# Summing the weighed chunks of a side scan by accumulating DMAs in place of VectorE additions

## The chip, the cores and the metric

The kernel runs on one core of a Trainium2 chip. The metric is the device time of one execution in microseconds (us); lower is better. All arrays are float32 unless it says otherwise.

## What is computed

Two layers on x of shape (8, 512, 128). Each is `x = x + s * silu(g)`, with s and g from the normalised x. In layer 0, s is a selective scan and g a mixture of eight experts, of which each token takes two. In layer 1, s is plain causal attention and g is a block with 16-head latent attention and another mixture of experts. The change touches the scan alone:

```python
z = sigmoid(x @ Wz + bz);  x_ssm = x @ Wx + bx
Bm = x @ WB + bB;  C = x @ WC + bC             # 16 states each
dt = softplus(x @ Wdt + bdt);  A_bar = exp(dt[..., None] * -exp(A_log))
x_db = x_ssm[..., None] * (dt[..., None] * Bm[..., None, :])
def ssm_step(h, inp):                          # over the 512 positions
    a_t, x_t, c_t = inp
    h_new = a_t * h + x_t
    y_t = einsum('bdn,bn->bd', h_new, c_t)     # the sum over the states
    return h_new, y_t
s = (y_ssm * z) @ Wout + bout
```

## The kernel before

The kernel has three stages. `route` normalises x, picks the experts and sorts tokens to them. `experts0` runs the experts of layer 0 over NT = 72 tiles of 128 tokens. `layer1` runs the whole second layer as a hand-written schedule of slots, 24 for each of the 8 batches; in every slot each engine finds by its loop what is due.

The scan of layer 0 is a side job, spread by hand over the stages that have other work. Batches 0 to 2 (SCANNED = 3) are scanned inside `experts0`, batches 3 to 7 inside `layer1`, shortly before layer 1 needs each of them. Features lie on the 128 partitions and positions along the row. A chunk is PER = 2 of the 16 states, so a batch has NC = 8 chunks, each a tile of 128 x 1024 float32, which is 512 KB. In `experts0` a chunk comes every three tiles, in `layer1` every four slots.

One chunk k of batch b takes these steps, with n = 8 b + k:

- GpSimd issues two loads (`load_rows`, L212) that spread the rows of B and of C from DRAM (`scan_bc`) over all partitions into `sc_bc_wide`, which has two buffers. The load for chunk n waits until chunk n-2 has used its rows.
- ScalarE makes the decays `sc_a` (L250).
- VectorE multiplies `sc_u` by the B rows into `sc_ub` (`enter`, L291), runs the recurrence into `sc_state` (`step`, L298), multiplies the state by the C rows (`weigh`, L308) and adds the product to the running sum `sc_y` (`add`, L315). The weighed chunk goes into `sc_ub`, which is free after the recurrence; that of chunk 0 goes straight to `sc_y`. The `enter` of the next chunk therefore waits for the `add` of this one.
- After the last chunk `gate` adds the two halves of `sc_y` (L320) and multiplies by the gate (L323). TensorE projects (L196), and `finish` (L327) takes the rows.

In `experts0` VectorE goes through tile m in this order: four products that give `hid` (L908), then `finish`, `add` of the chunk that is due three tiles back, `enter` of the chunk due now, `step` of the one due a tile back, `weigh` of the one due two tiles back. TensorE does the up projections of tile m (L767), the pieces of the scan, the down projections of tile m-2 (L776 and L778, which wait for `hid`), then turns the rows of tile m+2 (L758). SP fetches the expert weights of each tile (`wst`, 512 KB from `in_wexp` and 4 KB from `bias_cols`) into five buffers. GpSimd gathers the rows of the tiles (`xrow`, L885), eight tiles ahead, and issues the loads of the scan between them.

In `layer1` VectorE begins each slot with the maxima of one group of scores (`reduce_maxima`, L1676). TensorE's next scores (L1256, L1259) wait for these, since there is one bank pair for them. After it come the pieces of the scan and then whatever else is due. GpSimd issues the loads, the gathers of expert outputs (L1630) and small roots. SP issues small copies between the engines' steps: `q_all<-q_kind`, `dens<-o`, `rec_wide<-head_recips`.

## Time and profile before

| | us |
|---|---|
| median of 3 runs | 1355.73 |
| lowest, highest | 1346.55, 1360.17 |
| span of the profiled execution | 1355.0 |

| stage | from, to (us) |
|---|---|
| `route` and the start of `experts0` | 0 to 84 |
| `experts0` with the scan of batches 0 to 2 | 84 to 334 |
| end of `experts0`, start of `layer1` | 334 to 376 |
| `layer1` with the scan of batches 3 to 7 | 376 to 1116 |
| `layer1` without a scan | 1116 to 1355 |

The profile comes from one execution, whose own time is its span of 1355.0 us; the time around the span isn't given apart from it. The engines are PE (TensorE), PEld (its weight loads), DVE (VectorE), ACT (ScalarE), POOL (GpSimd) and SP. The chain that ended last is followed back from the end of the program. It does not go back beyond 345 us, where a barrier ends `experts0`; the first stages are read from waits and busy times instead.

### The profile page before, as it was taken

How to read it: one execution, taken by the hardware profiler on the slowest of the kernel's cores; microseconds unless marked ns; L12 is line 12 of the kernel's file. 1: busy time of each engine (PE TensorE's matmuls, PEld its weight loads, DVE VectorE, ACT ScalarE, POOL GpSimd, SP SyncE). 2: the span in 40 equal slices, each digit the busy share in tenths (PEclk: the TensorE clock that was granted, in tenths of full speed). 3: DMA queues.
4: the chain of work that ended last, by engine and by line, in shares of the span. 5: the costliest groups of instructions: out<-in, count | busy, mean ns of one | idle time of the engine just before them, and what ended most of it. 6: DMA issues, size and time to landing. Idle time of an engine off the chain costs nothing.

```text
span 1355.0 us, 21646 instructions
## 1 busy us (share of the span) xinstructions
PE 1197.1 (88%) x7528; PEld 720.3 (53%) x7528; DVE 989.3 (73%) x1648; ACT 641.1 (47%) x1309; POOL 282.1 (21%) x363
## 2 busy tenths in 40 slices
PE   7679989899778889898899989999989998998986
PEld 6568878788334334435544553553454455454353
DVE  6748877979487777986797896699889776653333
ACT  3657758575225334355336544454533533443421
POOL 1075434340303103202020320130032301000000
PEclk9779999999787689899799997999999988998799
DMA  7489978877253252253135323435333400310020
GB/s 196 159 279 295 297 238 285 276 254 230 102 125 96 70 117 85 86 115 101 60 95 134 109 76 86 115 98 105 105 93 95 125 25 18 56 41 18 17 49 8
DMA packets 99674, 167.06 MB, mean 123 GB/s; under 512 B 26216, under 2 KB 54448, under 8 KB 99504
## 3 DMA queue, kind: packets, MB, share of 16 engines
q1 hardware_dynamic: 76624, 89.37, 24.4%
q0 software_dynamic: 22784, 76.04, 18.0%
q8 instruction: 63, 1.03, 0.3%
q10 hardware_dynamic: 160, 0.26, 0.2%
q14 instruction: 43, 0.35, 0.1%
HBM read 141.37 MB, written 11.15 MB: 113 GB/s over the span
## 4 chain that ended last, share of the span: by engine, by line
PE 42%; DVE 17%; issue 6%; ACT 4%; DMA 4%; POOL 1%; SPq 0%; another core or an unknown queue 0%; DVEq 0%; POOLq 0%; ACTq 0%
PE bank L1219 9%; PE bank L1237 4%; PE bank L1256 4%; PE bank L1348 3%; PE bank L1295 3%; PE bank L1290 3%; PE bank L1286 3%; DVE neg_max L1676 3%; PE bank L1222 3%; PE bank L1259 2%; DVE sc_state L298 2%; PE bank L1277 2%; DMA rec_wide<-head_recips 2%; ACT probs L1486 1%; DVE sc_ub L291 1%
## 5 line engine op out<-in xcount | busy, mean ns | idle before, releaser
L1676 DVE TENSOR_REDUCE neg_max<-bank 128x2 f32<-128x1024 f32 (+3 forms) x256 | 204.2, 819 | 160.9 <-PE bank L1259 154.6
L1486 ACT ACTIVATE probs<-bank 128x1024 f32<-128x1024 f32 (+1 forms) x192 | 168.9, 880 | 316.9 <-PE bank L1222 290.6
L1219 PE MATMUL bank<-q_all,kk 49*128 49x512 f32 (+3 forms) x1024 | 221.8, 512 | 21.8 <-ACT probs L1486 18.9
L212 POOL DMA_DIRECT2D sc_bc_wide<-scan_bc x128 | 73.3, 574 | 496.3 <-DVE sc_ub L291 234.7
L767 PE MATMUL bank<-xcol,wst 128*128 128x128 f32 x1152 | 144.9, 280 | 1.6 <-DMA wst<-bias_cols 1.5
L298 DVE TENSOR_TENSOR_SCAN sc_state<-sc_a,sc_ub 128x1024 f32<-128x1024 f32 x64 | 145.9, 2280 | 0.0
L1256 PE MATMUL bank<-kr,q_all 48*128 48x512 f32 (+3 forms) x512 | 111.0, 430 | 33.5 <-DVE neg_max L1676 32.1
L767 PEld LDWEIGHTS bank<-xcol,wst 128*128 128x128 f32 x1152 | 138.3, 197 | 2.8 <-DMA wst<-bias_cols 2.8
L1219 PEld LDWEIGHTS bank<-q_all,kk 49*128 49x128 f32 x1024 | 81.4, 194 | 107.7 <-issue 54.1
L885 POOL DMA_INDIRECT xrow<-sorted_in,token_of x72 | 92.8, 1289 | 154.8 <-PE bank L758 105.9
L908 DVE SCALAR_TENSOR_TENSOR hid<-bank,wst,gel 128x128 f32<-128x128 f32 x288 | 80.3, 341 | 42.2 <-issue 40.3
L1256 PEld LDWEIGHTS bank<-kr,q_all 48*128 48x128 f32 x512 | 50.0, 192 | 104.5 <-DVE neg_max L1676 49.1
L1222 PEld LDWEIGHTS bank<-mask_t,ident 128*128 128x128 bf16 x512 | 29.4, 98 | 122.6 <-issue 115.4
L1237 PE MATMUL bank<-probs,vaug 128*32 128x512 f32 (+3 forms) x1024 | 94.4, 465 | 0.0
L836 ACT ACTIVATE gel<-bank,wst 128x128 f32<-128x128 f32 x288 | 81.5, 383 | 18.3 <-PE bank L767 17.6
L291 DVE TENSOR_TENSOR sc_ub<-sc_u,sc_bc_wide 128x1024 f32<-128x1024 f32 x64 | 78.0, 1218 | 15.4 <-DMA sc_bc_wide<-scan_bc 13.5
L250 ACT ACTIVATE sc_a<-sc_dt,neg_a 128x511 f32<-128x511 f32 x128 | 83.8, 710 | 5.8 <-PEq L680 5.3
L778 PE MATMUL bank<-w,hid 128*128 x576 | 84.9, 291 | 0.0
L1630 POOL DMA_INDIRECT expert_out<-sorted_out,slot x64 | 72.4, 1132 | 47.0 <-POOLq L138 26.9
L1259 PE MATMUL bank<-mask,ident 128*128 128x128 bf16 x512 | 75.8, 232 | 0.0
L1222 PE MATMUL bank<-mask_t,ident 128*128 128x128 bf16 x512 | 74.9, 229 | 0.0
L778 PEld LDWEIGHTS bank<-w,hid 128*128 128x128 f32 x576 | 71.0, 194 | 4.9
(295 smaller groups left out, 1834.8 us busy)
## 6 DMA issues: line engine op xcount, KB each, us to landing
sc_bc_wide<-scan_bc POOLq DMA_DIRECT2D x128, 512.0 KB
wst<-in_wexp SPq DMA_DIRECT2D x72, 512.0 KB
q_all<-q_kind SPq DMA_DIRECT2D x94, 128.0 KB, 4.4
rec_wide<-head_recips SPq DMA_DIRECT2D x31, 256.0 KB
p_t<-gates_turned SPq DMA_DIRECT2D x14, 512.0 KB
sorted_out<-xrow SPq DMA_DIRECT2D x7, 576.0 KB
rows_all<-in_x SPq DMA_DIRECT2D x8, 256.0 KB, 5.0
sorted_in<-rows_all SPq DMA_DIRECT2D x8, 256.0 KB, 5.8
```

The costliest lines, as they stand in the source:

```text
L291: self.nc.vector.tensor_tensor(v["ub"][:], v["u"][:].unsqueeze(1).to_broadcast([P, PER, L]), v["bc_wide"][:, n % 2, 0, :, :], ALU.mult).th ...
L298: self.nc.vector.tensor_tensor_scan(merged(v["state"][:]), merged(v["a"][:, n % 2, :, :]), merged(v["ub"][:]), 0.0, ALU.mult, ALU.add).the ...
L767: last = mm(bk(inner(m)[half])[:, f * P:(f + 1) * P], wst[:, m % WB, half * FF + f * P:half * FF + (f + 1) * P], xcol[:, m % 3, :], start= ...
L778: last = mm(bk(5)[:, 0:P], hid[:, m % 4, f, :], w2[:, bass.ds(e * FF + f * P, P)], start=False, stop=(f == FT - 1))
L885: nc.gpsimd.indirect_dma_start(out=xrow[:, m, :], out_offset=None, in_=xs[0:B * L], in_offset=bass.IndirectOffsetOnAxis(ap=t["token_of"][: ...
L1219: mm(bank[1][:, par, at:at + n], kk[rows, b % 2, kt * P:(kt + 1) * P], q_all[rows, quad // 2 % 3, pair, kt * P:L].bitcast(F32), start=True ...
L1222: last = mm(bank[1][:, par, at:at + P], t["ident16"][:], t["mask_t16"][:], start=False, stop=True)
L1237: last = mm(bk(4)[row:row + 32, kt * P:L], vaug[:, b % 2, kt, :], probs[:, (6 * quad + 2 * kg + pr) % RING, par, at:at + L - kt * P], star ...
L1256: mm(bank[0][:, par, at:at + n], q_all[rows, quad // 2 % 3, pair, i * P:(i + 1) * P], kr[rows, b % 2, 0:n], start=True, stop=False)
L1259: last = mm(bank[0][:, par, at + i * P:at + n], t["ident16"][:], t["mask16"][:], start=False, stop=True)
L1486: af(probs[:, slot % RING, :, 0:width], bank[1][:, :, 0:width], ACT.Exp, scale=0.125).then_inc(s["p_ready"], 1)
L1676: last = v.tensor_reduce(neg_max[:, quad % 2, pr:4:2, i], bank[0][:, :, at:at + (i + 1) * P], AX, ALU.max, negate=True)
```

## The change

For chunks 1 to 6 of every batch (ADDED = NC - 2 = 6) VectorE no longer adds. GpSimd issues a DMA that reads the weighed chunk and accumulates it into `sc_y`, in SBUF on both sides, 512 KB each (`accumulate`). Chunk 0 still writes `sc_y` directly. Chunk 7 is still added by VectorE (`add_last`), which waits for its product and for all six DMAs of the batch.

The weighed chunk gets a tile of its own, `sc_weighed`, so `enter` waits only for the recurrence of the chunk before. In turn `weigh` of chunk k, for k of 2 and up, waits until the DMA of chunk k-1 has landed (`sc_acc`), and each DMA waits for the one before it.

Place in GpSimd's order: in `experts0` behind the load of the C rows in the iterations 11 tiles after a chunk is due; GpSimd waits there for the `weigh` of that chunk. In `layer1` behind the load of the C rows in the slot where VectorE weighs the chunk one slot earlier in the schedule (`chunk_due(slot, 3)`).

To make room, three small tiles of `route` are laid over `sc_weighed`, and `turned_rows` in `layer1` is halved by packing.

```diff
+ADDED = NC - 2
@@ def scan_tiles
-        ub=sb("ub", [P, PER, L]), state=sb("state", [P, PER, L]), ...
+        ub=sb("ub", [P, PER, L]), weighed=sb("weighed", [P, PER, L]), state=sb("state", [P, PER, L]), ...
@@ def enter
         if k == 0:
             dve.wait_ge(s["sc_u"], b + 1)
-            if b >= 1:
-                dve.wait_ge(s["sc_add"], (NC - 1) * b)
-        if k == 1:
+        if n >= 1:
             dve.wait_ge(s["sc_scan"], n)
         dve.wait_ge(self.rows_in[0][n % 2], 16 * (n // 2 + 1))
-        if k >= 2:
-            dve.wait_ge(s["sc_add"], (NC - 1) * b + k - 1)
@@ def weigh
+        if k >= 2:
+            dve.wait_ge(s["sc_acc"], 16 * (ADDED * b + k - 1))
         dve.wait_ge(self.rows_in[1][n % 2], 16 * (n // 2 + 1))
-        to = v["ub"] if k >= 1 else v["y"]
+        to = v["weighed"] if k >= 1 else v["y"]
@@
-    def add(self, dve, b, k):
+    def accumulate(self, pool, b, k):
         s, v = self.s, self.v
-        dve.wait_ge(s["sc_hc"], b * NC + k + 1)
+        pool.wait_ge(s["sc_hc"], b * NC + k + 1)
         if k >= 2:
-            dve.wait_ge(s["sc_add"], (NC - 1) * b + k - 1)
-        self.nc.vector.tensor_tensor(v["y"][:], v["y"][:], v["ub"][:], ALU.add).then_inc(s["sc_add"], 1)
+            pool.wait_ge(s["sc_acc"], 16 * (ADDED * b + k - 1))
+        pool.dma_start(v["y"][:], v["weighed"][:], accum_op=ALU.add).then_inc(s["sc_acc"], 16)
+
+    def add_last(self, dve, b):
+        s, v = self.s, self.v
+        dve.wait_ge(s["sc_hc"], NC * (b + 1))
+        dve.wait_ge(s["sc_acc"], 16 * ADDED * (b + 1))
+        self.nc.vector.tensor_tensor(v["y"][:], v["y"][:], v["weighed"][:], ALU.add).then_inc(s["sc_add"], 1)
@@ experts0, gpsimd
                         if (at := chunk_due(m - after)) is not None and at >= (0, 2):
                             scan.load_rows(pool, *at, what)
+                    if (at := chunk_due(m - 11)) is not None and 1 <= at[1] <= ADDED:
+                        scan.accumulate(pool, *at)
@@ experts0, vector
-                    if (at := chunk_due(m - 3)) is not None and at[1] >= 1:
-                        scan.add(dve, *at)
-                        if at[1] == NC - 1:
-                            scan.gate(dve, at[0])
+                    if (at := chunk_due(m - 3)) is not None and at[1] == NC - 1:
+                        scan.add_last(dve, at[0])
+                        scan.gate(dve, at[0])
@@ layer1, gpsimd
                             scan.load_rows(pool, *at, what)
+                    if (at := chunk_due(slot, 3)) is not None and 1 <= at[1] <= ADDED:
+                        scan.accumulate(pool, *at)
@@ layer1, vector
-                    if (at := chunk_due(slot, 3)) is not None and at[1] >= 1:
-                        scan.add(dve, *at)
+                    if (at := chunk_due(slot, 3)) is not None and at[1] == NC - 1:
+                        scan.add_last(dve, at[0])
```

## Rows read from the trace of the kernel before

**Rows 1.** Busy time by stage: us, engine busy (instructions), PEclk, DMA share, GB/s.

```profile
core 0: us, PE busy (x) PEld busy (x) DVE busy (x) ACT busy (x) POOL busy (x), PEclk, DMA share, GB/s
84.00:334.00 250.00, 231.28 (x1829) 209.23 (x1828) 205.77 (x377) 174.58 (x497) 110.06 (x108) 0.99 0.86 275
...
376.00:1116.00 740.00, 670.56 (x4010) 339.28 (x4008) 597.47 (x848) 332.97 (x556) 135.68 (x178) 0.91 0.37 97
```

**Rows 2.** The additions, groups of VectorE instructions by line, whole program.

```profile
L315 DVE TENSOR_TENSOR sc_y<-sc_y,sc_ub 128x1024 f32<-128x1024 f32 x56 | 68.0, 1214 | 0.0
```

**Rows 3.** Waits between 80 and 343 us: us in total, times, longest.

```profile
DVE sc_ub L291 <- DMA sc_bc_wide<-scan_bc: 13.5, 1, 13.5
...
PE bank L758 <- DVE sc_rows L327: 5.4, 2, 2.7
...
PE bank L776 <- DVE hid L908: 3.8, 3, 1.4
...
PE bank L767 <- DMA wst<-bias_cols: 1.5, 2, 1.4
```

**Rows 4.** Waits over the whole program, longest in total first.

```profile
PEld bank L1256 <- DVE neg_max L1676: 49.1, 40, 3.7
...
PE bank L1256 <- DVE neg_max L1676: 32.1, 26, 3.5
```

**Rows 5.** Additions and batch ends on the chain that ended last: start, us.

```profile
444.30 1.13 DVE sc_y L315
...
692.39 1.22 DVE sc_y L315
...
802.65 1.22 DVE sc_y L315
...
809.90 0.61 DVE sc_y L320
...
1033.27 1.22 DVE sc_y L315
```

**Rows 6.** DMA in 84:334: queue rows, then issues with KB each.

```profile
DMA packets 36557, 68.73 MB, mean 275 GB/s; under 512 B 12829, under 2 KB 20893, under 8 KB 36524
...
q1 hardware_dynamic: 27727, 39.74, 48.7%
q0 software_dynamic: 8797, 28.58, 36.6%
...
wst<-in_wexp SPq DMA_DIRECT2D x67, 512.0 KB
sc_bc_wide<-scan_bc POOLq DMA_DIRECT2D x44, 512.0 KB
```

**Rows 7.** Short stretches of `experts0`, columns as in the first group.

```profile
80.00:86.00 6.00, 6.00 (x43) 5.81 (x43) 3.63 (x6) 2.64 (x11) 4.79 (x6) 0.80 1.03 381
...
194.00:206.00 12.00, 12.00 (x100) 11.10 (x99) 11.90 (x22) 6.85 (x22) 6.67 (x7) 1.00 0.91 289
```

**Rows 8.** A lone 512 KB load, KB and median us to landing.

```profile
c_wq<-in_wq SPq DMA_DIRECT2D x1, 512.0 KB, 4.1
```

**Rows 9.** VectorE between 84 and 165 us: start, us, line.

```profile
107.90 1.22 DVE L308 TENSOR_TENSOR sc_ub<-sc_state,sc_bc_wide 128x1024 f32<-128x1024 f32 x1
...
116.78 1.21 DVE L308 TENSOR_TENSOR sc_ub<-sc_state,sc_bc_wide 128x1024 f32<-128x1024 f32 x1
...
129.66 1.21 DVE L308 TENSOR_TENSOR sc_ub<-sc_state,sc_bc_wide 128x1024 f32<-128x1024 f32 x1
...
133.14 1.23 DVE L291 TENSOR_TENSOR sc_ub<-sc_u,sc_bc_wide 128x1024 f32<-128x1024 f32 x1
```

**Rows 10.** GpSimd's loads of the scan in `experts0`: start, us.

```profile
110.78 0.58 POOL L212 DMA_DIRECT2D sc_bc_wide<-scan_bc  x1
113.93 0.60 POOL L212 DMA_DIRECT2D sc_bc_wide<-scan_bc  x1
```

**Rows 11.** VectorE in `layer1`, two successive weighings of the scan: start, us.

```profile
688.29 1.22 DVE L308 TENSOR_TENSOR sc_ub<-sc_state,sc_bc_wide 128x1024 f32<-128x1024 f32 x1
...
708.63 1.22 DVE L308 TENSOR_TENSOR sc_ub<-sc_state,sc_bc_wide 128x1024 f32<-128x1024 f32 x1
```

**Rows 12.** The chain between 450 and 550 us, shares of the stretch by line.

```profile
by line: PE bank L1219 12.1%; issue 7.0%; PE bank L1256 6.5%; PE bank L1237 5.4%; DMA rec_wide<-head_recips 5.1%; DMA q_all<-q_kind 4.4%; PE bank L1259 4.2%; DMA dens<-o 4.2%; DVE neg_max L1676 3.5%; PE bank L1222 3.3%; DVE sc_state L298 3.
```

More of the change, by code:

```diff
@@ L172, in scan_tiles @@
         bc_wide=sb("bc_wide", [P, 2, 2, PER, L]),
-        ub=sb("ub", [P, PER, L]), state=sb("state", [P, PER, L]), y=sb("y", [P, PER, L]), rows=sb("rows", [P, 3, J, P]))
+        ub=sb("ub", [P, PER, L]), weighed=sb("weighed", [P, PER, L]), state=sb("state", [P, PER, L]), y=sb("y", [P, PER, L]), rows=sb("rows", [P, 3, J, P]))
 def merged(t):
@@ L351, in route @@
         rstd = sb("r_rstd", [P, T])
-        prob, left = sb("r_prob", [P, T, E]), sb("r_left", [P, T, E])
+        early = t["scan"]["weighed"][:].rearrange("p a b -> p (a b)").rearrange("p (n i e) -> p n i e", n=4, i=T)
+        prob, left, firsts = early[:, 0], early[:, 1], early[:, 2:4]
         small = sb("r_small", [P, T, 4])
-        firsts, order = sb("r_firsts", [P, 2, T, E]), sb("r_order", [P, E])
+        order = sb("r_order", [P, E])
         picked = sb("picked", [P, T, E])
@@ L896, in _ @@
                             scan.load_rows(pool, *at, what)
+                    if (at := chunk_due(m - 11)) is not None and 1 <= at[1] <= ADDED:
+                        scan.accumulate(pool, *at)
             @block.vector
@@ L1018, in layer1 @@
         neg_max = sb("neg_max", [P, 2, 4, J])
[L1019 to L1021 removed]
+        turned_rows = sb("turned_rows", [32 + J * E, L])
+        neg_max_t = turned_rows[0:4 * J, 0:2 * P].rearrange("p (q w) -> p q w", q=2)
+        gates_t, gates_rows = turned_rows[32:32 + E, :], turned_rows[32:32 + J * E, 0:P]
         probs = sb("probs", [P, RING, 2, L])
@@ L1622, in _ @@
                             scan.load_rows(pool, *at, what)
+                    if (at := chunk_due(slot, 3)) is not None and 1 <= at[1] <= ADDED:
+                        scan.accumulate(pool, *at)
                     if (b := due(slot, "gather")) is not None:
```

7 lines of the change are left out of this document (2 added, 5 removed).

## The prediction

> **What bounds the kernel now.** I read the busy time by stage first. Between 84 and 334 us TensorE is busy 231.3 of 250 us and VectorE 205.8, and the DMA engines 0.86 of the time [rows 1]. A clean stretch shows who sets the pace: in 12 us TensorE is busy all 12.00 and VectorE 11.90 [rows 7]. So TensorE bounds this stage, VectorE is all but level with it, and the DMA engines are not far off. Between 376 and 1116 us TensorE is busy 670.6 of 740 us, VectorE 597.5, the DMA engines only 0.37 [rows 1]. After 1116 us there is no scan, and nothing of the change reaches it.
>
> Next the waits, which say who holds TensorE up. In the first stage it waited for VectorE 5.4 us at the end of a batch and 3.8 us for `hid`, and 1.5 us for weights [rows 3]. Over the whole program its scores waited 32.1 us, 26 times, for VectorE's maxima; the weight loads' 49.1 us lie partly over the same gaps [rows 4]. That is what relief of VectorE can buy.
>
> Last the chain that ended last. It runs through seven additions between 444 and 1033 us, each 1.13 or 1.22 us [rows 5]. One of them, at 802.65, is the last of its batch, since the sum of the halves (L320) follows at 809.90. That one stays on VectorE, so six leave the chain.
>
> **What the change removes.** 48 of the 56 additions at 1.214 us [rows 2], 58.3 us of VectorE. Of these 18 fall into `experts0` (21.9 us) and 30 into `layer1` (36.4 us). All that VectorE has behind an addition starts 1.2 us sooner, where VectorE is late.
>
> In `experts0` TensorE is the bound, so the gain is at most its waits for VectorE, 5.4 + 3.8 = 9.2 us [rows 3], and at least nothing. The larger item lies at the batch ends, where the addition stays. I take 3 us.
>
> In `layer1` the six additions on the chain are 5 x 1.22 + 1.13 = 7.2 us. If VectorE had been on the path throughout its waits, the gain could reach the 32.1 us of [rows 4]; if TensorE is right behind, it falls towards nothing. Additions just off the chain help a little in the same crowded stretches. I take 10 us, near the chain's own count.
>
> **What it adds on the DMA engines.** 48 DMAs of 512 KB, SBUF to SBUF. The trace has no accumulating DMA. From below: the fastest stretch moves 381 GB/s [rows 7], at which 0.524 MB take 1.38 us of all 16 engines. From above: an accumulate reads the source, reads the destination and writes it. If those passes follow each other, it is three times that, 4.1 us. I take two passes, 2.75 us, as the writing can run beside the reading, and keep both ends.
>
> The Trainium skill bears on the value, in "Collectives: The Full Stack", section "The bandwidth ceiling: the fold count and why AG ≠ RS ≠ AR": an add in the DMA engine is slow because it reads two sources, and a reduce there ran at 32.35 GB/s beside 62.28 for a copy. By its ratio of 1.93 an accumulate would take an estimated 2.66 us here, and the sum would be lower by 18 x 0.09 = 1.6 us at the most. No row of this trace shows it.
>
> In `experts0`: the 68.73 MB of 84 to 334 us [rows 6] need 180 us at 381 GB/s, and 18 x 2.75 = 50 us come on top: 230 of 250 us. On average it fits; the point where it no longer does is (250 - 180) / 18 = 3.9 us each. A chunk has 250 / 24 = 10.4 us, and needs 180 / 24 + 2.75 = 10.3. A clean chunk is shorter: TensorE does 100 matmuls in 12 us [rows 7], some 25 or 26 a tile, so three tiles are 9.4 us. There the engines are 0.9 us short. Were every one of the 18 chunks clean, that would be 16 us; the gaps around them and five weight buffers absorb part.
>
> A rule of the skill speaks against the change here. "DMA: Bandwidth & Descriptors", section "Issuing engines are not separate DMA queues", says that DMAs from any engine end on the same 16 DMA engines and interleave. By it GpSimd's additions can't slip past the weights. By that rule the shortfall above is due, and the trace agrees as far as it can: the two queues hold 48.7% and 36.6% of the same 16 engines.
>
> **The waits it adds.** `weigh` of chunk k waits for the DMA of chunk k-1. In the tight case a weighing ends at 107.90 + 1.22 = 109.1 and the next begins at 116.78, which leaves 7.7 us; the next pair has 129.66 - 118.0 = 11.7 us [rows 9]. A lone 512 KB load took 4.1 us to land [rows 8]; with a second reading of 1.38 us it is 5.5. That fits alone. With the weights taking half the engines it can double to some 10, about 2 us late in the tight chunks. Behind a late `weigh` on VectorE stand `hid` of the next tiles and then TensorE's down projections, two tiles on. VectorE has 1.2 us more slack in each chunk, so I count half of it: 1 us in half of the 18 chunks is 9 us at the most. Shortfall and late waits are the same contention; together I take 7 us (from 0 to 16).
>
> GpSimd itself waits for the weighing: after the load at 110.78 until 118.0. Behind it stand two gathers, eight tiles ahead, and the load now at 113.93 [rows 10], which would go at some 120. Its rows are used at 133.14 [rows 9], so 13 us remain where 19 were. It needs the addition's 2.75, its own 1.4 and 2.7 of latency, 6.9 us, or 11 when shared. I cost this at nothing; what hides it is the two buffers. SP's queue is passed by nothing.
>
> In `layer1` two weighings are 20.3 us apart [rows 11], so the DMA has 19 us to land, and it stands behind a load that waits for the same weighing: no new wait on GpSimd. Its 30 x 2.75 = 83 us lift the DMA share from 0.37 to 0.48. The price is collision with small copies on the chain: they are 5.1 + 4.4 + 4.2 = 13.7% of it in one stretch [rows 12]. If each of the 30 delays such a copy by its whole length whenever one is there, that is 30 x 0.137 x 2.75 = 11 us; queues share, the chain has this density only in places, and the loads of 512 KB do the same already. I take 2 us (0 to 11). The issue on GpSimd is like a load's 0.6 us [rows 10], 29 us on an engine that is busy 110 of 250 and 136 of 740 us [rows 1]. The looser wait of `enter` and the packed tiles cost and bring nothing.
>
> **The sum.** 1355.0 - 3 + 7 - 10 + 2 = 1351.0 us, made against the span of the profiled execution, which is 0.7 us below the median of the runs, so it needs no correction.
>
> **The rivals.**
>
> *The relief is larger (0.26).* The accumulate costs little more than a copy, 1.38 us: then `experts0` needs 180 + 25 = 205 of 250 us and waits for nothing. VectorE's backlog in the crowded parts of `layer1` shrinks by more than the chain counts. For it: seven chain additions are only those that ended last. With 9 us in `experts0` and 18 in `layer1` (a little over half of the 32.1) the time is 1328 us. Against it: TensorE is busy over 90% anyway.
>
> *The accumulate is slow (0.32).* If one takes more than the 3.9 us worked out above, the DMA engines become the bound of `experts0`, and `weigh` waits in each chunk. At 6 us, 180 + 18 x 6 = 288 us, which is 38 us over the stage's 250; with `layer1` at 10 - 4 = 6 us better, the time is 1387 us. It is past 1% slower from about 5 us each. For it: no row shows an accumulate, and my upper end of 4.1 us is already past the point. Against it: the stage has gaps, and two readings at copy speed stay below.
>
> *About no change (0.42).* My forecast, from 1342 to 1368 us: relief and contention nearly cancel. It also holds the case in which TensorE takes up at once what VectorE frees.
>
> **How the numbers follow.** The likeliest gives 1351. A measurement of this kernel can tell about 1% (14 us) from no change. The range of 1330 to 1385 us takes in nearly all of the large relief and of the slow accumulate, and leaves about 2 in 10 outside. Faster by over 1%: 0.26, within 1%: 0.42, slower by over 1%: 0.32.
>
> **What would show it.** In the changed profile: VectorE's busy time down by 58 us; GpSimd with 48 more issues of 0.6 us or so; the DMA share of `experts0` up from 0.86 to near 1, and of `layer1` to about 0.48. The price of one accumulate shows in the packets of GpSimd's queue. A wait "DVE L308 <- DMA sc_y" in the tight chunks of `experts0` and none in `layer1` would bear out the deadlines. `experts0` should be 4 us longer and `layer1` 8 us shorter. I am wrong if such waits stand in `layer1`, if TensorE waits for weights for more than a few us, or if TensorE's 32.1 us for the maxima hardly move.

## The result

The changed kernel takes 1376.7 us in the median of 4 runs (1373.4 to 1380.2); beside it the kernel before took 1354.0 us (4 runs, 1346.6 to 1360.2). The ratio is 1.018, with a 95% interval from 1.013 to 1.023. The change makes the kernel about 25 us slower. That lies inside the wide range of 1330 to 1385 us, near its upper end, but the forecast was 4 us faster and the likeliest case about no change; both were wrong. The prediction had given 0.32 to "slower by over 1%".

The page of the changed kernel, its span, VectorE's and GpSimd's busy time, the DMA queue that GpSimd issues and the shares of the chain that ended last:

```profile
span 1378.4 us, 21646 instructions
...
PE 1202.7 (87%) x7528; PEld 720.6 (52%) x7528; DVE 936.7 (68%) x1600; ACT 642.8 (47%) x1309; POOL 332.9 (24%) x411
...
q0 software_dynamic: 29696, 101.21, 27.2%
...
PE 42%; DVE 12%; DMA 9%; issue 5%; ACT 4%; SPq 1%; another core or an unknown queue 1%; POOL 1%; POOLq 0%; ACTq 0%; DVEq 0%
```

Queue 0, which GpSimd issues, had 22784 packets, 76.04 MB and 18.0% before. The additions came: 6912 packets more, 48 x 144. VectorE is relieved too. The chain shows the exchange: VectorE's share fell from 17% to 12%, that of the DMAs rose from 4% to 9%.

The stages of the changed kernel, in the columns of [rows 1]:

```profile
84.00:334.00 250.00, 223.16 (x1716) 199.59 (x1714) 176.92 (x342) 168.81 (x474) 130.36 (x124) 0.98 0.97 303
376.00:1116.00 740.00, 660.80 (x3962) 333.29 (x3960) 559.44 (x813) 333.21 (x555) 162.09 (x209) 0.92 0.48 117
```

The DMA share went from 0.86 to 0.97 in `experts0` and from 0.37 to 0.48 in `layer1`. TensorE did 1716 matmuls in the first window where [rows 1] has 1829: the same 250 us hold less of the work. TensorE's mean granted clock is level with [rows 1] in `layer1` (0.92 beside 0.91) and a little lower in `experts0` (0.98 beside 0.99); the measure below shows what that is worth.

The waits of the changed kernel that matter (us in total, times, longest):

```profile
POOL sc_y L315 <- DVE sc_weighed L307: 93.5, 18, 20.8
...
PE bank L1266 <- DVE neg_max L1688: 32.0, 26, 3.5
DVE o L1748 <- DMA rec_wide<-head_recips: 31.9, 18, 4.0
...
DVE recs L1745 <- DMA dens<-o: 20.8, 7, 8.8
...
PE bank L1358 <- DVE o L1748: 15.7, 7, 3.5
...
PE bank L774 <- DMA wst<-bias_cols: 11.8, 13, 3.2
...
DVE sc_weighed L307 <- issue: 7.9, 6, 2.2
```

The same waits of the kernel before:

```profile
DVE recs L1733 <- DMA dens<-o: 15.6, 7, 9.0
...
DVE o L1736 <- DMA rec_wide<-head_recips: 14.3, 7, 4.2
...
PE bank L1348 <- DVE o L1736: 7.9, 7, 3.1
```

Three things are to be seen. TensorE's waits for the maxima did not move (32.1 us in [rows 4], 32.0 here). In `experts0` TensorE now waits for weights: 11.8 us where [rows 3] has 1.5. In `layer1` the attention's small copies come late (`rec_wide` 14.3 to 31.9 us), and TensorE's attention projection, which waits for `o`, waits 15.7 us where it waited 7.9.

For the experiments one more measure is needed: the length of `experts0` in a profile, from the weighing of chunk 0 to the first gather of the experts' output. Before, from the timeline:

```profile
87.76 1.21 DVE L308 TENSOR_TENSOR sc_y<-sc_state,sc_bc_wide 128x1024 f32<-128x1024 f32 x1
...
346.54 1.00 POOL L1630 DMA_INDIRECT expert_out<-sorted_out,slot  x1 [26.95 <-POOLq L138]
```

and after:

```profile
84.86 1.22 DVE L307 TENSOR_TENSOR sc_y<-sc_state,sc_bc_wide 128x1024 f32<-128x1024 f32 x1
...
356.49 1.06 POOL L1642 DMA_INDIRECT expert_out<-sorted_out,slot  x1 [18.94 <-POOLq L139]
```

That is 258.8 us before and 271.6 us after. Divided at these points, each kernel does the same work on either side, and TensorE's idle time is the length less its busy time (the ends of its matmuls are modelled, so only differences count). The kernel before in two rows, then the changed one, in the columns of [rows 1]:

```profile
87.76:346.54 258.78, 234.68 (x1836) 211.71 (x1835) 210.33 (x384) 174.78 (x498) 106.79 (x107) 0.98 0.82 262
346.54:1355.00 1008.46, 904.98 (x5382) 458.87 (x5381) 722.70 (x1089) 426.45 (x713) 155.15 (x208) 0.91 0.31 81
...
84.86:356.49 271.63, 239.75 (x1831) 214.66 (x1831) 189.79 (x366) 174.75 (x496) 130.58 (x124) 0.97 0.92 285
356.49:1378.40 1021.91, 908.77 (x5382) 459.23 (x5381) 690.58 (x1059) 427.71 (x713) 181.87 (x238) 0.90 0.39 95
```

In `experts0` the idle time goes from 24.1 to 31.9 us and the busy time of the same matmuls from 234.7 to 239.8; in `layer1` the idle time goes from 103.5 to 113.1. All this comes from one execution each, so it is read over many kernels below.

### The profile page after: what moved, and what is told of

Same layout as the page of the kernel before. It is cut to its first block, busy times and chain, and to the rows that moved or that the text cites. A ratio compares the mean times of both kernels' runs of the same rounds, so it can differ in the third digit from the quotient of the medians.

```text
span 1378.4 us, 21646 instructions
## 1 busy us (share of the span) xinstructions
PE 1202.7 (87%) x7528; PEld 720.6 (52%) x7528; DVE 936.7 (68%) x1600; ACT 642.8 (47%) x1309; POOL 332.9 (24%) x411
## 3 DMA queue, kind: packets, MB, share of 16 engines
q1 hardware_dynamic: 76624, 89.37, 23.6%
## 4 chain that ended last, share of the span: by engine, by line
PE 42%; DVE 12%; DMA 9%; issue 5%; ACT 4%; SPq 1%; another core or an unknown queue 1%; POOL 1%; POOLq 0%; ACTq 0%; DVEq 0%
PE bank L1229 10%; PE bank L1247 4%; DMA rec_wide<-head_recips 4%; PE bank L1266 4%; PE bank L1358 3%; PE bank L1232 3%; PE bank L1300 2%; PE bank L1305 2%; PE bank L1269 2%; DMA head_recips<-recs 2%; PE bank L1296 2%; PE bank L1287 2%; ACT probs L1496 2%; DVE neg_max L1688 2%; DVE sc_state L295 1%
## 5 line engine op out<-in xcount | busy, mean ns | idle before, releaser
L774 PE MATMUL bank<-xcol,wst 128*128 128x128 f32 x1152 | 148.9, 285 | 11.9 <-DMA wst<-bias_cols 11.8
L892 POOL DMA_INDIRECT xrow<-sorted_in,token_of x72 | 99.5, 1382 | 87.7 <-remote 36.5
L1232 PEld LDWEIGHTS bank<-mask_t,ident 128*128 128x128 bf16 x512 | 29.5, 98 | 123.4 <-issue 116.4
L288 DVE TENSOR_TENSOR sc_ub<-sc_u,sc_bc_wide 128x1024 f32<-128x1024 f32 x64 | 77.9, 1218 | 15.0 <-DMA sc_bc_wide<-scan_bc 15.0
```

The source lines that it names most:

```text
L774: last = mm(bk(inner(m)[half])[:, f * P:(f + 1) * P], wst[:, m % WB, half * FF + f * P:half * FF + (f + 1) * P], xcol[:, m % 3, :], start= ...
L892: nc.gpsimd.indirect_dma_start(out=xrow[:, m, :], out_offset=None, in_=xs[0:B * L], in_offset=bass.IndirectOffsetOnAxis(ap=t["token_of"][: ...
L1232: last = mm(bank[1][:, par, at:at + P], t["ident16"][:], t["mask_t16"][:], start=False, stop=True)
```

## The experiments

Theory A: the DMAs' time on the shared 16 engines makes the kernel slower, at two places: weights come late in `experts0`, small copies come late in `layer1`. Theory B: the new waits do it (a weighing behind a DMA, GpSimd behind a weighing). Theory C: the relief is missing because VectorE's additions were never on the path.

All numbers together. "Ratio" is to the kernel before, timed beside it, with its 95% interval. The other columns come from the one profile of each kernel: the length of `experts0`, TensorE's waits for weights there, VectorE's for `rec_wide`, TensorE's for the attention's `o`, and TensorE's idle time in `experts0` and behind it. All are us.

| kernel | DMAs in experts0 / layer1 | ratio | experts0 | weights | rec_wide | o | idle, experts0 | idle, layer1 |
|---|---|---|---|---|---|---|---|---|
| before | 0 / 0 | 1 | 258.8 | 1.5 | 14.3 | 7.9 | 24.1 | 103.5 |
| changed | 18 / 30 | 1.0183 (1.0134 to 1.0232) | 271.6 | 11.8 | 31.9 | 15.7 | 31.9 | 113.1 |
| r_changed | 18 / 30 | 1.0189 (1.0152 to 1.0226) | 275.5 | 12.1 | 37.8 | 17.0 | 31.9 | 114.2 |
| e1_dma_experts | 18 / 0 | 1.0080 (1.0043 to 1.0117) | 267.7 | 9.5 | 15.9 | 8.6 | 29.5 | 99.9 |
| e2_dma_layer1 | 0 / 30 | 1.0062 (1.0030 to 1.0094) | 257.2 | 5.3 | 34.8 | 17.2 | 24.3 | 112.5 |
| e3_no_add | none, no addition | 0.9945 (0.9917 to 0.9973) | 258.3 | 4.4 | 16.1 | 10.1 | 24.0 | 103.6 |
| e4_own_tile | 0 / 0 | 1.0025 (0.9994 to 1.0056) | 260.8 | 2.8 | 15.7 | 8.0 | 23.2 | 97.9 |
| r_e4_own_tile | 0 / 0 | 0.9986 (0.9934 to 1.0037) | 260.0 | 3.3 | 14.4 | 7.9 | 23.6 | 106.7 |
| e5_traffic_apart | 18 / 30, no weighing waits | 1.0123 (1.0061 to 1.0184) | 273.1 | 13.8 | 37.4 | 17.8 | 34.6 | 113.2 |
| e6_plain_copy | 18 / 30 copies | 1.0068 (1.0034 to 1.0101) | 266.7 | 5.3 | 26.2 | 11.9 | 27.4 | 109.9 |
| e7_gpsimd_add | GpSimd adds | 1.0236 (1.0193 to 1.0278) | 263.1 | 2.6 | 15.1 | 10.1 | 24.7 | 117.9 |
| e8_off_copies | 0 / 10 | 0.9983 (0.9953 to 1.0013) | 259.2 | 2.7 | 18.2 | 11.6 | 23.7 | 103.8 |
| r_e8_off_copies | 0 / 10 | 0.9980 (0.9955 to 1.0006) | 256.5 | 2.1 | 15.9 | 10.9 | 23.2 | 105.2 |
| e9_on_copies | 0 / 10 | 1.0002 (0.9969 to 1.0036) | 261.0 | 3.2 | 26.8 | 11.8 | 23.9 | 104.4 |
| r_e9_on_copies | 0 / 10 | 0.9993 (0.9961 to 1.0026) | 257.8 | 4.3 | 26.6 | 12.1 | 24.5 | 103.8 |
| e10_at_dens | 0 / 10 | 1.0095 (1.0056 to 1.0135) | 256.8 | 1.4 | 28.7 | 18.5 | 22.7 | 114.6 |
| r_e10_at_dens | 0 / 10 | 1.0042 (1.0012 to 1.0072) | 257.3 | 4.7 | 22.1 | 15.5 | 24.4 | 111.4 |
| e11_half_experts | 9 / 0 | 1.0080 (1.0041 to 1.0119) | 268.1 | 11.9 | 17.5 | 10.5 | 28.6 | 103.0 |
| e12_odd_experts | 9 / 0 | 1.0037 (0.9999 to 1.0074) | 266.2 | 7.0 | 14.6 | 8.3 | 28.0 | 103.7 |
| e13_two_thirds | 0 / 20 | 1.0004 (0.9958 to 1.0050) | 253.8 | 2.0 | 27.3 | 9.6 | 23.0 | 111.9 |

Two readings of the table serve below. The kernels without a DMA in `experts0` show waits for weights of 1.4 to 5.3 us, so only more than that is news. Twelve of them also have no addition on GpSimd; their idle time in `experts0` lies between 22.7 and 24.5 us, mean 23.7, while their stage lengths scatter from 253.8 to 261.0. That scatter is TensorE's busy time for the same work: 230.8 us at a mean granted clock of 1.00 in the shortest, 237.6 us at 0.96 in one of the longest.

In every kernel but the repeat of the changed one, two small functions choose who adds a chunk; the rest is the changed kernel.

```diff
+def by_dma(b, k):
+    return 1 <= k <= NC - 2 and b < 3          # e1
+def by_vector(b, k):
+    return k == NC - 1 or 1 <= k and not by_dma(b, k)
...
-                    if (at := chunk_due(m - 11)) is not None and 1 <= at[1] <= ADDED:
+                    if (at := chunk_due(m - 11)) is not None and by_dma(*at):
                         scan.accumulate(pool, *at)
```

**The changed kernel again.** No edit.

> The changed kernel once more, on the same chip as the next ones. If the prices add up, its ratio to before is the relief of e3_no_add (0.9945) plus 10 us in experts0 and 16 us in layer 1 (e2_dma_layer1 less e3_no_add), which makes 1.0137. If the parts make each other worse, 1.018 or more, as in its first measurement.

1.0189: the slowdown is real and is known to within 0.4%. It stands over the 1.0137 that the added prices gave; by the words above the parts would make each other worse. Those prices have intervals of their own, and the next paragraph says how far that goes.

**The DMAs in one stage only.** The edit above; for the second kernel `b >= 3`.

> The chunks of batches 0 to 2 are added by DMA, those of batches 3 to 7 by VectorE again. Theory A (contention in both stages): the profile of the changed kernel has the first expert gather 10 us later than before and the rest 13 us longer, so this one is about 10 us slower than before (1364, ratio 1.007). Theory B (all of the loss comes from the stage whose DMA engines are full): some 23 us slower (1377). Theory C (the loss is in layer 1 alone, and experts0 only drifts between executions): within 3 us of before.

> The chunks of batches 3 to 7 are added by DMA, those of batches 0 to 2 by VectorE. Theory A: the 30 DMAs collide with the small copies that layer 1 waits for, and this costs more than VectorE's relief of 10 us brings; about 10 to 13 us slower than before (1366). Theory B: 8 us faster, as predicted (1347). Theory C: some 20 us slower.

Each stage alone is slower: 0.8% (about 11 us, as theory A expected) and 0.6% (about 8 us, where 10 to 13 had been expected). The marks stay with their stage. With DMAs in `experts0` only, the stage is 267.7 us and `rec_wide` waits 15.9 us, as before; with DMAs in `layer1` only, the stage is 257.2 us and `rec_wide` waits 34.8 us. The two excesses add up to 1.4% where the whole change shows 1.8 and 1.9%. The intervals allow this to be no difference; nothing measured here says more.

**No addition at all.** Chunks 1 to 6 are weighed, and neither VectorE nor a DMA adds them, so the running sum holds only chunks 0 and 7.

```diff
+def by_dma(b, k):
+    return False
+def by_vector(b, k):
+    return k == NC - 1
```

> The additions of chunks 1 to 6 are left out in every batch, by VectorE and by DMA, so the running sum holds chunks 0 and 7 only. It is VectorE's relief without its price. Theory A (the prediction's term was right): 3 + 10 = 13 us faster than before, 1342. Rival (TensorE takes up at once what VectorE frees): within 4 us of before, 1350 to 1357. Rival (the relief is larger, but contention ate it): 25 us faster or more, 1330.

The ratio is 0.9945, that is 7.4 us faster (3.6 to 11.2 from the interval), between the 13 us and the 4 us that had been expected. This is what taking 58 us off VectorE brings when nothing else has to carry them. `experts0` is 258.3 us with 24.0 us of idle time, so nothing of it is seen there. In `layer1` its profile shows no less idle time either (103.6 us, beside 97.9 to 106.7 in six kernels in which VectorE adds), so where the 7 us lie is not known. And TensorE's waits for the maxima are not what was won, as its list of waits shows:

```profile
PE bank L1288 <- DVE neg_max L1710: 34.1, 27, 3.5
```

**Tile and packing alone.** `by_dma` returns False and VectorE adds every chunk, from the tile of its own.

> VectorE adds all chunks as before; only the tile of its own for the weighed chunk, its looser wait in enter and the packed small tiles stay. Theory A: these cost and bring nothing, ratio 1.000 within the noise of 0.3%. Rival: the new placement in SBUF or the other waits cost something themselves, 5 us or more.

> e4_own_tile again, as the level from which the thirds start: 1.000 to 1.003 if the first value holds. If it is 1.000 or under, the relief that e3_no_add shows is the 7 us against before and not the 11 us against e4_own_tile.

1.0025 and 0.9986: nothing that can be told from 1. The packed tiles and the looser wait cost and bring nothing that shows. As the repeat is under 1.000, the relief is counted as the 7 us against the kernel before.

**The traffic without the waits.** The additions are left out as above, and 48 accumulating DMAs of the same size run at the same places, from the running sum into a tile that nobody reads. No weighing waits for one but that of chunk 0, for those of the batch before. The product goes back to `sc_ub`, and `enter` waits for the weighing before it. GpSimd still waits for each weighing before it issues the DMA, as in the changed kernel (88.3 us in all, beside 93.5), so this tests one of the two waits of theory B.

```diff
 def weigh
-            dve.wait_ge(s["sc_acc"], 16 * (ADDED * b + k - 1))
+            dve.wait_ge(s["sc_hc"], n)
-        to = v["weighed"] if k >= 1 else v["y"]
+        to = v["ub"] if k >= 1 else v["y"]
 def accumulate
-        pool.dma_start(v["y"][:], v["weighed"][:], accum_op=ALU.add).then_inc(s["sc_acc"], 16)
+        pool.dma_start(v["weighed"][:], v["y"][:], accum_op=ALU.add).then_inc(s["sc_acc"], 16)
```

> The additions of chunks 1 to 6 are left out on VectorE, as in e3_no_add, and the 48 accumulating DMAs are issued at the same points with the same size, but add the running sum into a scratch tile that nobody reads. No weighing waits for them. Theory A (the traffic itself costs, by slowing the weights in experts0 and the small copies in layer 1): about as slow as the changed kernel, ratio 1.015 to 1.018 to before. Rival W (the new wait of the weighing for the DMA costs): near e3_no_add, ratio 0.995 to 1.000.

1.0123, a little under the 1.015 to 1.018 of theory A and well over the rival, with every mark of the changed kernel: `experts0` 273.1 us, `rec_wide` 37.4 us, and these waits:

```profile
PE bank L1385 <- DVE o L1775: 17.8, 7, 4.3
...
PE bank L800 <- DMA wst<-bias_cols: 13.8, 9, 4.5
```

Against the kernel without additions (0.9945) the traffic, with GpSimd's wait, costs 1.0123 - 0.9945 = 1.8%, some 24 us. What is left for the weighing's wait is 1.0189 - 1.0123 = 0.7%, with an interval of the one figure alone of 0.6% to each side, so by the medians it is the smaller part and may be nothing. GpSimd's wait has no trace behind it: VectorE's waits for the rows of the scan are 15.0 us in the changed kernel beside 13.5 before, and TensorE's for the gathered tiles 9.0 beside 9.3. Leaving that wait out alone was not tried.

**The same DMAs as plain copies.** Everything waits as in the changed kernel, only the DMA overwrites instead of accumulating, so the sum isn't made.

```diff
-        pool.dma_start(v["y"][:], v["weighed"][:], accum_op=ALU.add).then_inc(s["sc_acc"], 16)
+        pool.dma_start(v["y"][:], v["weighed"][:]).then_inc(s["sc_acc"], 16)
```

> The changed kernel with plain copies of the weighed chunk over the running sum in place of the accumulates, all waits kept; so the sum is not made. Packets should take 0.16 us in place of 0.33. Theory A (time on the DMA engines is the price): about half of the price of e3_no_add to the changed kernel goes, ratio 1.005 to 1.008. Rival W (waits and places in the queues are the price, whatever the length): 1.013 to 1.018.

The queue's row on the page of this kernel, whose span is 1353.3 us:

```profile
q0 software_dynamic: 29696, 101.21, 23.2%
```

and of its waits TensorE's for the attention's `o` and for weights:

```profile
PE bank L1380 <- DVE o L1770: 11.9, 7, 2.9
...
PE bank L795 <- DMA wst<-bias_cols: 5.3, 4, 2.8
```

The same packets and bytes take less of the engines. The issue is shorter too, 0.56 us on GpSimd in place of 0.95. Of all 16 engines a copy costs (0.232 x 1353.3 - 0.180 x 1355.0) / 48 = 1.46 us, an accumulate (0.272 x 1378.4 - 0.180 x 1355.0) / 48 = 2.73 us. The ratio falls from 1.0189 to 1.0068: at an unchanged set of waits, half the engine time takes back 1.2%, some 16 us. That is theory A again, and it leaves little for the waits: the copy's price over the kernel without additions is 1.0068 - 0.9945 = 1.2%, half of the changed kernel's 2.4%, as 1.46 us is half of 2.73. The figures come from shares given to a tenth of a per cent, and kernels without these DMAs differ by a few us in the queue's total, so each is good to about 0.1 us. They are means over both stages: by the same reckoning the eighteen in `experts0` alone take about 2.5 us each and the thirty in `layer1` alone about 3. The ratio of 2.73 to 1.46 is 1.87. The Trainium skill's "Collectives: The Full Stack", section "The bandwidth ceiling: the fold count and why AG ≠ RS ≠ AR", has a measured ratio of 1.93 between an AllGather, which copies, and a ReduceScatter, which adds. This case agrees with it within that accuracy.

**GpSimd adds itself.** No DMA; GpSimd does the addition as an instruction, with the same waits.

```diff
-        pool.dma_start(v["y"][:], v["weighed"][:], accum_op=ALU.add).then_inc(s["sc_acc"], 16)
+        self.nc.gpsimd.tensor_tensor(v["y"][:], v["y"][:], v["weighed"][:], ALU.add).then_inc(s["sc_acc"], 1)
```

> The additions of chunks 1 to 6 as an instruction of GpSimd on the same tiles, at the places of the DMAs. No DMA traffic, and VectorE is relieved. Theory A (traffic is the price): near e3_no_add, ratio 0.995 to 1.000. Rival G (GpSimd's own adding holds up VectorE's instructions or its own queue of gathers and loads): VectorE's instructions on two tiles in SBUF get longer than 1.22 us and the time is slower than before by 0.5% or more.

1.0236, the slowest of all, as rival G had it. Its groups by line, GpSimd's addition and one of VectorE's products (busy us, mean ns of one, idle before):

```profile
L335 POOL TENSOR_TENSOR sc_y<-sc_y,sc_weighed 128x1024 f32<-128x1024 f32 x48 | 121.8, 2537 | 65.0 <-DVE sc_weighed L319 64.6
```

```profile
L300 DVE TENSOR_TENSOR sc_ub<-sc_u,sc_bc_wide 128x1024 f32<-128x1024 f32 x64 | 90.5, 1414 | 14.6 <-DMA sc_bc_wide<-scan_bc 14.6
```

An addition takes GpSimd 2.54 us, and VectorE's products with the B rows rise to 1414 ns from 1218. Its weighings, which GpSimd's addition waits for, stay at 1213 ns. TensorE's waits for the maxima rise to 38.6 us and its idle time in `layer1` to 117.9, the most of all. How the 2.4% splits between these is not known. The Trainium skill ("SBUF — State Buffer", section "Who interferes with whom") says that a VectorE instruction with two SBUF inputs contends with a GpSimd instruction that reads SBUF. The longer products are what that would look like; the trace does not show the cause itself.

**Ten DMAs in `layer1`, by place.** The slots of `layer1` come in groups of six, one per step of the attention. The 30 chunks fall on three places of a group, ten each. These kernels give one place to the DMAs, VectorE adds the other 20.

```diff
 def by_dma(b, k):
-    return 1 <= k <= NC - 2
+    return 1 <= k <= NC - 2 and b >= 3 and (4 * (8 * (b - 3) + k) - 11) % 6 == 5   # 3 for e9, 1 for e10
```

> Only ten chunks of layer 1 are added by DMA, those whose DMA goes out in a slot that is 5 modulo 6, when no small copy of the reciprocals is under way; all others by VectorE. Theory A (collision with dens, recs and rec_wide is the price in layer 1): VectorE waits for rec_wide 15 to 18 us as before, and the time is that of e4_own_tile, 1.000 to 1.003. Rival T (any traffic in layer 1 costs the same): a third of the price of e2_dma_layer1, ratio 1.003 to 1.005, and rec_wide's wait at 21 us.

> Only ten chunks of layer 1 are added by DMA, those whose DMA goes out in a slot that is 3 modulo 6, just as the reciprocals are spread. Theory A: VectorE's wait for rec_wide rises to 25 us or more (from 15), that is most of the rise that e2_dma_layer1 shows with thirty DMAs, and the ratio is 1.004 to 1.008. Rival T: the same as e8_off_copies in time and in the wait.

> Only ten chunks of layer 1 are added by DMA, those whose DMA goes out in a slot that is 1 modulo 6, the slot of the copy of the denominators (dens); all others by VectorE. The third third of e2_dma_layer1, after e8_off_copies (slots 5) and e9_on_copies (slots 3). Theory A (small copies are hit when a DMA goes out with them): VectorE's waits for dens or rec_wide rise, by 5 us or more over e4_own_tile's 17.5 and 15.7 us, and the ratio is 1.002 to 1.005. Rival T: as e8_off_copies, 0.998, waits as there.

> e8_off_copies again, beside the other two thirds on one chip. Theory A: 0.997 to 1.001. Rival N (differences of half a per cent between these kernels are scatter from one call to the next): a value outside of that.

> e9_on_copies again. If its first value of 1.000 holds although VectorE waits 11 us longer for rec_wide than with VectorE's additions, then a late rec_wide costs little by itself. If it rises to 1.004 or more, the first value was scatter.

> e10_at_dens again. Theory D (a DMA in the slot of the denominators is the dear one, as it delays the whole chain of copies and the attention that waits for it): 1.006 to 1.012 again, well over the other two thirds. Rival N: it comes back to 1.002 to 1.004.

Each was measured twice. At places 5 and 3 the ratio is 0.998 and 1.000. At place 1 it is 1.0095, over the 1.002 to 1.005 expected, and then 1.0042, under the 1.006 to 1.012 expected of the repeat; both are clear of 1. TensorE's idle time in `layer1` says the same: 103.8 to 105.2 us at places 5 and 3, 114.6 and 111.4 at place 1, where all thirty give 112.5 to 114.2. At place 3 VectorE's waits for `rec_wide` rise as theory A expected, to 26.8 us, but the ratio does not:

```profile
DVE o L1770 <- DMA rec_wide<-head_recips: 26.8, 16, 4.1
...
PE bank L1380 <- DVE o L1770: 11.8, 7, 2.8
```

At place 1, the slot in which the attention's row sums are copied (`dens`), the wait for `rec_wide` is about the same, but TensorE now stands behind `o`:

```profile
DVE o L1770 <- DMA rec_wide<-head_recips: 28.7, 16, 4.3
...
PE bank L1380 <- DVE o L1770: 18.5, 7, 3.9
```

The copies before `rec_wide` tell the two places apart. In the kernel with place 3, `head_recips` (8 KB, on which `rec_wide` depends) has only loads ahead of it, and `rec_wide` follows 1.4 us later; in the kernel with place 1 an accumulate has gone out beside the same loads, 4.9 us ahead of it, and `rec_wide` follows after 4.2 us:

```profile
995.73 0.34 SPq L1161 DMA_DIRECT2D head_recips<-recs  x1
997.11 0.56 SPq L1166 DMA_DIRECT2D rec_wide<-head_recips  x1
...
1001.26 1.02 POOL L335 DMA_DIRECT2D sc_y<-sc_weighed  x1
...
1006.11 0.34 SPq L1161 DMA_DIRECT2D head_recips<-recs  x1
1010.35 0.56 SPq L1166 DMA_DIRECT2D rec_wide<-head_recips  x1
```

It is the same at two more such copies of the trace: 1.4 us each without the accumulate, 4.2 and 3.3 with it. At place 1 `o` has no time in hand: in the kernel before, VectorE began it 5.4 us after the issue of these three `rec_wide`, which is about the time of the copy. At nine of the ten places 3 it began 5.7 to 9.1 us after the issue, at seven of them 7.3 or more, so that a copy of 8 us mostly still came in time. So the number of late copies does not set the cost; the time in hand behind each does.

**Twenty DMAs in `layer1`, without place 1.** The condition becomes `% 6 != 1`.

> The twenty chunks of layer 1 whose DMA goes out in a slot that is 3 or 5 modulo 6 are added by DMA; the ten of slot 1 and all of experts0 by VectorE. It is the version that the experiments point to. Theory D (the slot of the denominators and experts0 hold the whole price): TensorE's wait at the attention's projection stays at 12 us or less and the ratio is 0.995 to 0.999, a little faster than before. Rival T (traffic in layer 1 adds up, whatever the slot): 1.001 to 1.005.

1.0004 (0.9958 to 1.0050), TensorE behind `o` 9.6 us. Leaving out ten of the thirty gives back by the medians about what the 30 had cost (1.0062), but the intervals overlap, and the gain that theory D expected (0.995 to 0.999) isn't seen. Its profile speaks against it too: 111.9 us of idle time in `layer1`, nearly that of all thirty, and a short `experts0` of 253.8 us at a granted clock of 1.00.

**Nine DMAs in `experts0`.** `by_dma` takes chunks 2, 4, 6 of a batch, or 1, 3, 5.

```diff
-    return 1 <= k <= NC - 2 and b < 3
+    return k in (2, 4, 6) and b < 3            # (1, 3, 5) for e12
```

> In experts0 only chunks 2, 4 and 6 of each batch are added by DMA, nine in all; all others and layer 1 by VectorE. Theory S (the DMA engines are over-full only where their spare time is used up, so the price is convex): experts0 is 0 to 3 us longer than with VectorE's additions, ratio 1.001 to 1.004. Rival L (each DMA has the same price): experts0 4 to 6 us longer, half of what the eighteen cost, ratio 1.005 to 1.007.

> In experts0 only chunks 1, 3 and 5 of each batch are added by DMA, the complement of e11_half_experts, whose nine DMAs already made experts0 as long as all eighteen do. Theory P (the even ones are dear since the load of rows and the weights after them come in a tight place): experts0 is 0 to 4 us longer than with VectorE's additions (259 us), ratio 1.001 to 1.004. Rival S (either nine fill the DMA engines in the dense stretches, and the next nine fall into stalls that are there already): 6 to 9 us longer, ratio 1.006 to 1.009.

The stage is 268.1 and 266.2 us long, beside 267.7 to 275.5 with eighteen DMAs and a mean of 258.1 with none. The 10 us of the first are more than either view had said (0 to 3, 4 to 6), the 8 us of the second lie in rival S's range. The ratios have less to say: 1.0080 and 1.0037, beside 1.0080 with eighteen. TensorE's waits for weights, in the list of waits of the kernel with chunks 2, 4, 6, and then in that of the kernel with 1, 3, 5:

```profile
PE bank L795 <- DMA wst<-bias_cols: 11.9, 10, 4.5
```

```profile
PE bank L795 <- DMA wst<-bias_cols: 7.0, 8, 1.8
```

Over all kernels the stage length sorts by traffic. The twelve profiles with no DMA and no GpSimd addition in `experts0` lie between 253.8 and 261.0 us, mean 258.1. The two with nine have a mean of 267.2, the four with eighteen accumulates 272.0, the one with eighteen copies 266.7. By length, nine accumulates cost about 9 us and eighteen about 14, which looks as if the first were dearer. TensorE's idle time shows that they aren't: over the mean of 23.7 us it grows by 4.6 us with nine (28.6 and 28.0), by 8.3 with eighteen (29.5 to 34.6) and by 3.7 with eighteen copies. That is about 0.5 us for each accumulate and 0.2 for each copy. The rest of the length is busy time for the same matmuls:

```profile
85.35:353.48 268.13, 239.50 (x1831) 215.59 (x1831) 199.66 (x375) 174.39 (x496) 119.51 (x116) 0.96 0.86 270
```

This is the kernel with chunks 2, 4, 6. The seven kernels with DMAs in `experts0` have busy times of 238.2 to 243.5 us at a granted clock of 0.95 to 0.97, all twelve without 230.8 to 237.6 us at 0.96 to 1.00. So some 4 of the nine us and some 6 of the fourteen are slower work that goes with a lower clock. Whether the DMAs bring the clock down by making TensorE idle more, no run shows. The two sets of nine chunks come out too near each other to say that a chunk's place counts.

## Why the prediction was wrong, and where it was right

The terms of the traffic failed: +7 us in `experts0`, where the runs show 11 to 14, and +2 us in `layer1`, where they show about 16. The relief, -13 us in all, was 7. The forecast had the sign wrong because it set the first two so low.

**The price of one accumulate: right.** 2.75 us of all engines was predicted, 2.73 measured. The rival "the accumulate is slow" needed more than 3.9 us to decide and is refuted, although the time ended on its side: the slowdown came at a price at which the prediction had said that it fits.

**VectorE's relief in busy time: about right.** 989.3 to 936.7 us is 52.6 less, where 58 were said; the issue on GpSimd was dearer than said:

```profile
L315 POOL DMA_DIRECT2D sc_y<-sc_weighed x48 | 45.4, 945 | 93.5 <-DVE sc_weighed L307 93.5
```

0.95 us each instead of 0.6. Nothing shows that this cost anything, nor GpSimd's 93.5 us of waiting, but no run takes either away alone. The load that was to go out later by some 6 us was costed at nothing, and VectorE's waits for such loads bear that out (15.0 us beside 13.5).

**Relief in `experts0`, predicted -3 us: nothing.** Without any addition the stage took 258.3 us, beside a mean of 258.1, with 24.0 us of TensorE's idle time, beside 23.7. TensorE bounds the stage, as the prediction itself had read.

**Contention in `experts0`, predicted +7 us: about +14 by the stage lengths, +11 by the ratio.** This step failed in size. "On average it fits" compared 230 us of engine time with 250 us of stage, where the 180 us for the traffic that was there came from the rate of the fastest stretch, 381 GB/s. [rows 1] had the share itself, 0.86, which is 215 us; with 50 us for the DMAs that is an estimated 265 us, 15 too many, and the point where it no longer fits is (250 - 215) / 18 = 1.9 us each and not 3.9. The prediction then worked out a sharper figure, 0.9 us short in a clean chunk, 16 us in all, and took half. Both figures lie near the measured 11 to 14 us, but in part by luck: the engines were not full on average (a share of 0.92 over the changed stage), and of the 14 us some 8 are idle time of TensorE and some 6 its busy time at a lower clock, for which the prediction has no term. The runs also show no threshold: nine DMAs, half the load, already cost 4.6 us of idle time, at a DMA share of 0.86 over their stage. Of each accumulate's 2.73 us about 0.5 (8.3 / 18) reached TensorE as idle time and 0.8 (14 / 18) the stage.

**The waits for the DMA: small.** The forecast wait of a weighing on a DMA isn't named so in the waits; VectorE's idle time before L307 for which no releaser shows is 7.9 us, 6 times, with 2.2 us at most, of the size that was said for a late DMA ("about 2 us"). The landing was forecast well too, 5.5 us alone and some 10 when shared: in the kernels with DMAs in one stage only, the median from issue to landing is 7.9 us in `experts0` and 6.8 us in `layer1`. The prediction counted late waits and the shortfall as one. The traffic without the weighing's waits shows that the shortfall carries most of it: weights late for TensorE by 13.8 us (11.8 in the changed kernel), which the prediction had named as a sign that it would be wrong.

**Relief in `layer1`, predicted -10 us: about -7, way unknown.** The kernel without additions won 7.4 us (3.6 to 11.2). That this is the chain's count of 7.2 may be luck, since its profile doesn't show where they were won. The upper bound of 32.1 us from the waits for maxima was no bound of anything: they stayed at 32.0 with the DMAs and 34.1 without any addition. The additions don't stand ahead of those waits. The large relief, a rival with 0.26, is refuted with it: it needed 27 us, and the interval of the kernel without additions ends at 11. The unmoved 32.1 us had been named as a sign of being wrong, like the late weights.

**Collisions in `layer1`, predicted +2 us: about +16.** The largest miss. It follows from 1.0062 with the DMAs and 0.9945 without any addition: 1.17% or 15.8 us for 30 DMAs, some 10 to 22 us by the intervals; the new waits of `layer1` are in it. By the median it is even above the upper end given, 11 us. That bound multiplied the copies' share of the chain before, 13.7%, by the length of a DMA, as if the chain would stay. It didn't: copies that ended just ahead of other work before, and so were not on it, came onto it. Between 376 and 1116 us the chain before holds `rec_wide` once. The small copies on the chain of the changed kernel (start, us) from 550 us on:

```profile
552.16 4.35 DMA head_recips<-recs
...
556.53 5.19 DMA rec_wide<-head_recips
...
580.61 1.33 DMA head_recips<-recs
581.95 8.64 DMA rec_wide<-head_recips
...
671.88 3.68 DMA head_recips<-recs
675.58 4.80 DMA rec_wide<-head_recips
...
697.39 1.35 DMA head_recips<-recs
698.76 8.07 DMA rec_wide<-head_recips
```

It holds `rec_wide` eight times, 47 us in all. Two of the eight took 8.64 and 8.07 us, the others 4.7 to 5.8. Ahead of six of them `head_recips` took 3.3 to 4.4 us, where its median before is 1.4; four of these six are copies behind an accumulate at place 1, and in the kernel before the same four took 2.7, 1.4, 1.4 and 1.4 us. What lay beside the first of the two long ones shows in GpSimd's timeline of the changed kernel:

```profile
580.43 0.55 POOL L213 DMA_DIRECT2D sc_bc_wide<-scan_bc  x1 [5.76 <-DVE sc_weighed L307]
580.98 0.93 POOL L315 DMA_DIRECT2D sc_y<-sc_weighed  x1
```

A load and an accumulate, 1 MB together, are released by the same weighing, within half a microsecond of each other, and just ahead of the copy at 581.95. The copy at 698.76 has the same pair ahead of it. A load alone does not do it. In the kernel before, five such copies of 256 KB went out 1.3 to 1.6 us behind a load alone, and `o` began 5.4 to 5.7 us after them without a wait for them, as here:

```profile
748.94 0.54 POOL L212 DMA_DIRECT2D sc_bc_wide<-scan_bc  x1 [11.02 <-DVE sc_ub L308]
...
750.48 0.54 SPq L1134 DMA_DIRECT2D rec_wide<-head_recips  x1
...
756.22 0.68 DVE L1736 TENSOR_TENSOR o<-o,rec_wide 128x512 f32<-128x512 f32 x1
```

The prediction had seen that the DMA stands behind a load that waits for the same weighing, and had drawn from it only that GpSimd gets no new wait. That the two go out as one burst into the copies follows from the same sentence, and wasn't drawn.

What stays open: TensorE's direct waits behind `o` grew by only 8 to 10 us. The other 6 to 8 of the 16 us are not attributed. That the ten DMAs at place 1 carry the cost is shown by the two kernels with them alone (1.0095 and 1.0042, idle time as with all thirty). The kernel without them (1.0004) agrees in time but not in idle time, so what the other twenty cost is open.

**The sum.** With the measured terms it is 0 + 14 - 7 + 16 = 23 us beside the 25 measured, or 20 with the 11 us of the ratio. A second count, from the profiles, needs no difference of ratios. TensorE's idle time grew by 8.3 us in `experts0`. In `layer1` it is 112.5 to 114.2 us in the four kernels with thirty accumulates, mean 113.2, and 97.9 to 106.7 in the six in which VectorE adds, mean 102.4: 10.8 us more, relief included. The busy time in `experts0` grew by 5.6. That makes 24.7 us; the busy time in `layer1` is left out, since it runs from 882 to 909 us over all kernels that don't add on GpSimd, whoever adds. The mechanisms were named but for the clock; the two prices of traffic were too low by 4 to 7 and by 14 us. Theory A carries the loss, theory C the 6 us by which the relief fell short of 13, and what is left for theory B is small by the medians.

No version that makes the whole sum beats the kernel before by more than the measurement can tell. The nearest is the one with ten DMAs at place 5, 0.998 twice, each interval taking in 1.

## What to carry to other kernels

Moving work from an engine to the DMA queues is not free because the queues have an average share to spare: take the share of the DMA engines that is in use from the profile and not from the rate of the fastest stretch, look at the tightest stretch of a stage and at the small copies on which a waiting engine depends, and take the full shortfall, not half. First measure the ceiling, by leaving the work out: here that was 7 us for 58 us of VectorE's time, less than doing all of them elsewhere cost in either way tried. The total of a wait ("TensorE waits 32 us for VectorE") bounds the gain only from work that stands directly ahead of it.

## What the chip showed that was not expected

An accumulating DMA of 512 KB in SBUF took 2.73 us of the 16 engines, a copy of the same packets 1.46 us. In a stage whose DMA share was 0.82 from end to end, TensorE's idle time grew by about 0.5 us with each such DMA, with nine as with eighteen; there was no free part at the beginning. TensorE's granted clock was lower in those stages too, 0.95 to 0.97 beside 0.96 to 1.00, and the same matmuls took about 5 us more. A copy of 256 KB that took 4.7 to 5.8 us took 8.1 and 8.6 us behind a burst of 1 MB, and one of 8 KB that took 1.4 us took 3.3 to 4.2 when an accumulate had gone out some 5 us ahead. GpSimd's addition of 128x1024 f32 took 2.54 us, twice VectorE's 1.21 us, and with 48 of them in the kernel VectorE's products with the B rows rose from 1218 to 1414 ns in the mean.
